# Side rows of the windowed distances: from four matmuls per group on tables built by three engines to one matmul of 316 columns on rows loaded from memory

## The reference, cut to what matters

```python
k_windows = q_h[:, idx, :]                 # the last 64 positions of every query
diff = k_windows - q_h[:, :, None, :]
dist = jnp.sqrt((diff * diff * m_h).sum(axis=-1) + 1e-08)
dist = jnp.where(mask[None], dist, jnp.inf)
neg_d, loc = jax.lax.top_k(-dist, K)       # K = 32
...
context = jnp.einsum('btk,btkd->btd', infl, neighbor_v)
```

## Time and profile before

| | us |
|---|---|
| median of 3 runs | 787.54 (785.96 to 788.2) |
| the profiled execution | 788.22 |
| its span | 786.4 |
| PE busy | 704.6 (90%) |
| DVE busy | 640.7 (81%) |
| POOL busy | 451.9 (57%) |
| ACT busy | 419.7 (53%) |

### The profile page before, as it was taken

How to read it: one execution, slowest core, us unless ns; L and a number is a source line. 1 busy time by engine, 2 the same in 40 slices (tenths; PEclk the granted TensorE clock), 3 DMA queues, 4 the chain that set the end, 5 groups by cost and what they waited for, 6 DMA issues and landing times.

```text
span 786.4 us, 11674 instructions
## 1 busy us (share of the span) xinstructions
PE 704.6 (90%) x3368; PEld 500.7 (64%) x3368; DVE 640.7 (81%) x2562; ACT 419.7 (53%) x757; POOL 451.9 (57%) x535
## 2 busy tenths in 40 slices
PE   3998999999999889999998999999998999978733
PEld 2645666666576666776676677666675776768623
DVE  3877787768999999849799999765799899659974
ACT  3754444566675555455675774456683754465300
POOL 2265366546676864854567856654668768433441
PEclk9979999999997999999998999999999999996555
DMA  9920000000000000000000000001000000010000
GB/s 287 358 68 1 1 0 0 2 1 16 17 1 10 9 15 11 9 15 20 13 1 8 11 12 16 8 7 26 14 2 9 10 15 15 19 31 8 18 23 17
DMA packets 25695, 22.14 MB, mean 28 GB/s; under 512 B 1892, under 2 KB 23424, under 8 KB 25120
## 3 DMA queue, kind: packets, MB, share of 16 engines
q1 hardware_dynamic: 25632, 21.40, 9.1%
HBM read 19.17 MB, written 2.23 MB: 27 GB/s over the span
## 4 chain that ended last, share of the span: by engine, by line
PE 44%; DVE 35%; POOL 7%; ACT 5%; issue 5%; DMA 4%; SPq 0%; DVEq 0%; POOLq 0%; ACTq 0%
PE bank_A L505 11%; PE bank_X L505 11%; PE bank_U L505 10%; PE bank_G L505 9%; DVE Wk L1193 8%; DVE S L790 6%; DVE m L1190 6%; DMA vw<-vscratch 4%; DVE GWk L790 2%; DVE sm L794 1%; POOL wT L1501 1%; POOL Wlo L1501 1%; ACT Ed L1259 1%; DVE wT L790 1%; ACT L1264 1%
## 5 line engine op out<-in xcount | busy, mean ns | idle before, releaser
L505 PE MATMUL bank_A<-S,WdT 128*128 128x512 f32 x368 | 186.8, 612 | 5.9 <-POOL S L1501 4.4
L1501 POOL TENSOR_TENSOR Wlo<-Wgu,Whi 128x256 fp32r<-128x256 f32 x138 | 108.3, 789 | 108.8 <-ACT Whi L1259 108.4
L790 DVE TENSOR_TENSOR S<-S,bank_U 128x512 f32<-128x512 f32 x184 | 123.7, 678 | 56.9 <-PE bank_U L505 36.0
L1259 ACT ACTIVATE S<-bank_G 128x512 f32<-128x512 f32 x184 | 108.2, 594 | 106.7 <-PE bank_G L505 98.0
L1501 POOL TENSOR_TENSOR S<-S,Rb 128x512 f32<-128x512 f32 x88 | 117.8, 1340 | 63.3 <-DVE S L790 59.3
L1259 ACT ACTIVATE Whi<-Wgu 128x256 fp32r<-128x256 f32 x184 | 74.0, 413 | 78.7 <-PE bank_U L505 69.8
L505 PE MATMUL bank_G<-xH,Whi 128*128 128x512 f32 x184 | 96.9, 526 | 5.5 <-POOL Wlo L1501 2.8
L505 PEld LDWEIGHTS bank_A<-S,WdT 128*128 128x128 f32 x368 | 66.7, 193 | 49.9 <-issue 29.2
L505 PE MATMUL bank_U<-xH,Whi 128*128 128x512 f32 x184 | 91.7, 498 | 5.0 <-DVE S L790 4.6
L790 DVE TENSOR_TENSOR S<-S,Rb 128x512 f32<-128x512 f32 x88 | 83.4, 951 | 2.4 <-ACT Rb L1259 0.5
L1193 DVE MATCH_REPLACE8 Wk<-m,Wk 128x79 f32<-128x79 f32 x384 | 81.8, 223 | 0.0
(11 more groups left out here) (233 smaller groups left out, 1440.9 us busy)
## 6 DMA issues: line engine op xcount, KB each, us to landing
vw<-vscratch SPq DMA_DIRECT2D x32, 158.0 KB
Wgu<-in_Wgu SPq DMA_DIRECT2D x2, 2048.0 KB, 15.3
xs<-in_x SPq DMA_DIRECT2D x4, 256.0 KB, 7.0
wqk<-in_w_qkv SPq DMA_DIRECT2D x1, 1024.0 KB, 7.3
Wgu<-in_Wgu SPq DMA_DIRECT2D x1, 1024.0 KB, 9.6
vscratch<-mo SPq DMA_DIRECT2D x4, 256.0 KB
out<-xs SPq DMA_DIRECT2D x3, 256.0 KB, 2.3
Wgu<-in_Wgu SPq DMA_DIRECT2D x1, 512.0 KB, 5.1
```

The lines of the kernel that those rows point to most:

```text
L505: return engine.matmul(dst, lhsT, rhs, start=start, stop=stop)
L790: return engine.tensor_tensor(dst, a, b, op)
L1259: return engine.activation(dst, src, f, bias=bias, scale=scale, accum_out=acc)
L1501: return engine.tensor_tensor(dst, a, b, op)
```

## The change

The queries' norms and the windows of key norms are no longer built by engines. Pk (now 8 rows) is stored to a scratch in DRAM, and for each group SP loads from it 4 rows of La (one per block, a piece of 16 values per head) and 8 rows of Ra (one per head, 4 windows of 79 values). La becomes one table of 28 rows and 128 columns for the whole group: 4 rows of query norms, 8 that pick the head, 16 that pick the query in the block. Ra has 28 rows of 4 by 79: 4 that are one in their own block only, 8 of key norms, 16 of the mask. PE issues one matmul of 316 columns, La against Ra, and then the four of Qb on top of it. `keys` on ACT is gone, and `operands` on DVE and POOL keeps Qb alone. SP gets a step `k`: the store of Pk, then two loads per group, from the third group on when the distances of the group two before are done. All strings of ORDER are written anew. The fixed rows of La and Ra come in 6 loads at the start in place of 4.

```diff
-AUX = 72
+AUX = GT + NH + TQ
...
     "sp":
-        "vvvvvvvvvsvvvvvvvvvsvvvvvvvvvsvvvvvsvvsvvss",
+        "vvvkkkkkkkkkvvvvvvsvvvkkkkkkkkkvvvvvvsvvvkkkkkkkkkvvvvvvvsvvkkkkkkkkvkvvsvvsvss",
...
+            def sides():
+                for b in range(B):
+                    yield
+                    sp.wait_ge(empty(bank("nm", b)), nth("nm", b) + 1)
+                    sp.wait_ge("pk", b + 1)
+                    load("st_p", pd[b], Pk[:, :])
+                    for g in range(NG):
+                        k, t0 = g % 2, g * GT * TQ
+                        yield
+                        if g == 0:
+                            sp.wait_ge("st_p", 16 * (b + 1))
+                        if g >= 2:
+                            sp.wait_ge(full(bank("dist", b, g - 2)), nth("dist", b, g - 2) + 1)
...
+                        q = pd[b, :, PADK + t0:]
+                        load(f"ld_s{k}", La[k][0:GT, :].rearrange("a (h t) -> a h t", h=NH),
+                             bass.AP(q.tensor, q.offset, [[TQ, GT], [PADK + T, NH], [1, TQ]]))
+                        q = pd[b, :, t0:]
+                        load(f"ld_s{k}", Ra[k][GT:GT + NH, :, :],
+                             bass.AP(q.tensor, q.offset, [[PADK + T, NH], [TQ, GT], [1, WK]]))
...
-                    pe.wait_ge("la_v" if not side else "la_p", side_count(not side, b, g))
-                    pe.wait_ge("ra", b * NG + g + 1)
+                    pe.wait_ge("qb_v" if queries_on_vector(b, g) else "qb_p", query_count(b, g))
+                    pe.wait_ge("ld_e", 96)
+                    pe.wait_ge(f"ld_s{k}", 32 * (b * (NG // 2) + g // 2 + 1))
+                    mm(t[:, 0:GT * WK], La[k][:, :], flat(Ra[k]), True, False)
                     for i in range(GT):
-                        o = t[:, WK * i:WK * i + WK]
                         w = slice(g * GT * TQ + TQ * i, g * GT * TQ + TQ * i + WK)
-                        mm(o, Qb[k][:, i, :], mk2[:, w], True, False)
-                        p = mm(o, La[k][:, i, :], Ra[k][:, i, :], False, True)
+                        p = mm(t[:, WK * i:WK * i + WK], Qb[k][:, i, :], mk2[:, w], False, i == GT - 1)
```

More of the change, by code:

```diff
@@ L73 @@
 _at = 0
-for _n, _w in (("ident", 128), ("bd", 128), ("tri", 64), ("neglo", 1), ("ones", 128), ("heads", AUX), ("pick", 128),
+for _n, _w in (("ident", 128), ("bd", 128), ("tri", 64), ("neglo", 1), ("ones", 128), ("heads", NH),
                ("eps8", 1), ("sel", 128)):
@@ L94, in constants @@
     h = np.arange(NH)
[L95 to L101, removed]
+    put("heads", p[:, None] // HD == h[None, :])
     put("sel", (p[:, None] % 16 == p[None, :] // 8) * 1.0)
@@ L317, in program @@
         hb = sb("hb", [64, 1])
-        nm72 = sb("nm72", [128, AUX])
-        Pk = sb("Pk", [AUX, PADK + T])
-        La = [sb(f"La{i}", [AUX, GT, 128]) for i in range(2)]
+        nm8 = sb("nm8", [128, NH])
+        Pk = sb("Pk", [NH, PADK + T])
+        La = [sb(f"La{i}", [AUX, 128]) for i in range(2)]
         Ra = [sb(f"Ra{i}", [AUX, GT, WK]) for i in range(2)]
@@ L376, in blocks_done, with queries_on_vector, query_count @@
             return b * NF + NF - NR + BLOCK * k + BLOCK - 1
-        def queries_on_vector(g):
+        def queries_on_vector(b, g):
             return g % 2 == 1
-        def side_count(on_vector, b, g):
-            return b * (NG // 2) + g // 2 + 1
+        def query_count(b, g):
+            on = queries_on_vector(b, g)
+            return sum(queries_on_vector(p, q) == on for p in range(B) for q in range(NG) if (p, q) <= (b, g))
         def last_side(b, g):
@@ L492, in stores @@
                             store(b, i, 1)
-            weave("sp", v=values(), s=stores())
+            weave("sp", v=values(), k=sides(), s=stores())
             sp.wait_ge("st_out", 16 * (B - 1 + NT))
@@ L1153, in operands @@
                     k, t0 = g % 2, g * GT * TQ
+                    if not queries_on_vector(b, g):
+                        continue
                     yield
@@ L1439, in head @@
                 if b > 0:
-                    sc_.wait_ge("ra", b * NG)
-                    sc_.wait_ge("la_p", b * NG // 2)
-                    sc_.wait_ge("la_v", b * NG // 2)
-                emptied(act(Pk[:, PADK:], t[0:AUX, :], ACT.Copy), "nm", b)
-            def keys(b):
-                for g in range(NG):
-                    k, t0 = g % 2, g * GT * TQ
-                    yield
-                    sc_.wait_ge("pk", b + 1)
-                    sc_.wait_ge("ld_e", 64)
-                    if g >= 2:
-                        sc_.wait_ge(full(bank("dist", b, g - 2)), nth("dist", b, g - 2) + 1)
-                    w = Pk[64:64 + NH, t0:t0 + WK]
-                    w = bass.AP(w.tensor, w.offset, [list(w.ap[0]), [TQ, GT], [1, WK]])
-                    act(Ra[k][64:64 + NH, :, :], w, ACT.Copy).then_inc(sems("ra"), 1)
+                    sc_.wait_ge("st_p", 16 * b)
+                emptied(act(Pk[:, PADK:], t[0:NH, :], ACT.Copy), "nm", b)
             def near(b):
@@ L1492, in scalar_engine @@
             weave("act", x=highs(), e=silus(), m=sums(), y=every(route), s=every(spreads), c=scales(), u=setup(),
-                  a=every(attend), f=every(dense), h=every(head), k=every(keys), n=every(near), g=every(gather))
+                  a=every(attend), f=every(dense), h=every(head), n=every(near), g=every(gather))
         def gpsimd_engine(engine):
```

118 lines of the change are left out of this document (54 added, 64 removed).

## The result

The changed kernel takes **813.8 us** (median of 4, 809.9 to 819.3) against 787.9 us for the kernel before beside it: a ratio of **1.034, 95% interval 1.026 to 1.041**. The forecast was 788.5 us and its range ended at 799, so it was wrong: slower, by some 26 us. The profiled execution took 817.1 us, its span is 815.3.

The account below looks back on a forecast made before the run. PE and DVE, both nearly full, bound the stretches beside the experts; serial window loads set the tail's end. Terms -8.6 - 2.4 - 3 + 7.5 + 1.5 + 1 + 5 = +1.0 gave 788.5 us as median, range 774 to 799.

Parts of the forecast that it names:

- The mechanism that it named: At batch heads, Pk's store and first side loads wait behind window loads, arriving 24.1 us after the values' store.
- PE's standstill: Before batch 2's first distances PE would stand 7.5 us waiting for side loads; batches 0 and 1 were covered.
- The third rival: Slower: from the third group on, every group waits on PE for its side loads; 801 us, chance 0.17.
- The standstill's price: Batch 2's head: 7.5 us of PE wait plus 1.5 us for a lower clock after it.
- what the change earns, -14 us: Beside the experts: savings of 8.6 us from PE's columns, 2.4 from the tables and 3 from the clock.
- PE's columns: One 316-column product at 0.53 us replaces four side products per group, saving 8.6 us over 24 groups, bounds 0.7 to 16.
- The clock's -3: Fewer, longer PE products beside the experts would win back 3 us of lost clock, bounds 0 to 8.6.
- the tables (-2.4): Table builds dropped from DVE, POOL and ACT would save 2.4 us of PE idle time, bounds 0 to 9.7.
- the tail, +5 us: After the experts, choosing starts 10.7 us later, leaner DVE regains part, and context 2 ends 5 us later.
- DVE's gain of 5.7 us: In the tail, DVE without table builds would get from first choice to context 2 in 30 us, before 35.7.
- four window loads carry every delay to the end: In the tail, four serial window loads take the 36 us to the end and pass on context 2's 5 us delay.
- the waits of later groups: From the third group on, pairs of side loads cost 0.3 us at three places a batch, 1 us in all.

Follow-up runs that it names:

- e1: Changed kernel, first two window loads of every batch cut into 64 and 15 rows: 800.5 us, ratio 1.016 to the kernel before.
- e5h: Changed kernel with engines in the order of the kernel before, first two window loads per batch cut into 64 and 15 rows: 796.5 us, ratio 1.010.
- e7n: Changed kernel, engines in the earlier kernel's order, 79-row windows, norm store and side loads on ACT's own queue: 801.3 us, ratio 1.014.
- e5e: Changed kernel, engines in the earlier kernel's order, without Pk's store and side loads (norms left out), 79-row windows: 780.2 us, ratio 0.989.
- e5ew: Changed kernel, engines in the earlier kernel's order, without Pk's store and side loads, all windows cut into 64 and 15 rows: 775.5 us, ratio 0.982.
- e3: Kernel before, with all window loads cut into 64 and 15 rows: 783.2 us, ratio 0.995.
- e2: Changed kernel, its own new order, all window loads cut into 64 and 15 rows: 794.2 us, ratio 1.005.
- e4: Changed kernel, its own new order, without Pk's store and side loads (norms left out): 805.7 us; one execution took 792.0.
- e5n: Changed kernel with engines in the order of the kernel before, all transfers kept, 79-row windows: 808.1 us, ratio 1.021.
- e5w: Changed kernel with engines in the order of the kernel before, all window loads cut into 64 and 15 rows: 793.5 us, ratio 1.004.
- e10w: Changed kernel, engines in the earlier kernel's order, windows cut into 64 and 15 rows, 316-column product behind its group's other four: 783.1 us, ratio 0.991.
- e12: e10w with one MLP product step moved ahead of the first distances on PE in batches 0 to 2: 782.5 us, ratio 0.991.
- e13: e12 with the attention-output step also moved ahead of the first distances in batch 3: 784.3 us, ratio 0.993.
- e8: e5w with the norms stored twice in each batch, the second store after the first has landed: 815.4 us, ratio 1.029.
- e7w: e7n with all window loads cut into 64 and 15 rows: 795.0 us, ratio 1.007.
- e9b: e5w without the norm store, side rows loaded straight from Pk in SBUF by five transfers a group: 812.8 us, ratio 1.024.

## Why the prediction was wrong

**The mechanism that it named was right.** The store lands under the window loads, and the first side tables were put at the values' store + 24.1: measured +24.8 from the values' store to the first distances of batch 3 (729.34 - 704.59), +25.1 in batch 2. PE's standstill was put in batch 2 alone of the first three, and it was there, 5.6 us for 7.5. The third rival, that every group waits for its loads, was not seen: only the heads wait. The Trainium skill, "DMA: Bandwidth & Descriptors", section "Why a DMA increments its semaphore by 16 and not by 1", has a DMA use the largest number up to 16 that divides its outermost sizes; by that 79 rows go on one engine and 64 on 16. The runs fit: cut into 64 and 15 rows the first windows let the norms through (e1, e5h), and without the cut not even another queue does (e7n, batch 3).

**The standstill's price was about right too.** The forecast had 7.5 us of wait and 1.5 of clock behind it, 9 in batch 2. Against e1, the same kernel with no wait there, batch 2 to 3 is 8.0 us longer for a wait of 5.6: 2.4 beyond its length, with a mean clock of 0.98 against 1.00. The 2.6 us for each us of the old-order runs is another case, of short waits at every head.

**First failed step: what the change earns, -14 us.** The largest term was PE's columns, -8.6. I took the proportion to the 512-column product, 0.53 us. It is 0.73 from start to next start, the other four cost 0.24 each instead of 0.22, and the term is 1.9 us, not far from its own lower bound of 0.7. The clock's -3 is nothing: from mo of batch 0 to mo of batch 3 the mean granted clock is 0.98 before, 0.98 in e5e and e5ew, and 0.97 in the changed kernel. With the tables (-2.4) the forecast had -14 us by the last head; e5e and e5ew, with nothing to fetch, have 2.9 and 4.2 (mo of batch 3 at 673.6 and 672.3 against 676.5). Over the whole kernel that gain is 8 us (e5e), and 10 us where both sides have wide windows (e5ew and e3, ratios 0.982 and 0.995, on different chips).

**Second, and not in the sum at all: the order.** I priced what is issued, not that every engine's order was written anew. Between batches 2 and 3 the new order takes 163.2 us with no wait for norms (e1, e2, e4), the old order with nothing to fetch 156.5 (e5e) and the kernel before 156.1: 7.1 us. The held store adds 8.0; together the 15.0 us. Which engine's string loses them no run separates.

**Third: the tail, +5 us.** It is +13.7. The first choice came 32.0 us after the values' store (736.57 - 704.59) where I had 28.7, and DVE's gain of 5.7 us was 1.1: from the first choice to the end are 78.7 us after and 79.8 before. Half of the 13.7 is the held store: e1, in the same order and with 0.2 us of such waits, has a tail of 116.5 us, 7.1 less than the changed kernel, and 6.6 more than before. In the old order the fetching alone makes as much: e5n's tail is 123.2 us, e5e's, with nothing to fetch, 107.6 and e5w's, with wide windows, 108.3. PE's waits for DMAs before (first line) and in e5n show that those for windows are the same and those for Ra came on top:

```profile
PE bank_U L505 <- DMA vw<-vscratch: 8.5, 2, 4.4
```
```profile
PE bank_G L524 <- DMA Ra<-pscratch: 12.6, 2, 10.0
PE bank_U L524 <- DMA vw<-vscratch: 8.4, 2, 4.4
```

The prediction also let four window loads carry every delay to the end, from two pieces of the chain of 15.4 and 15.0 us. PE's own waits for windows are 8.5 us in all, and without them the kernel before gains 0.5%, some 4 us (e3).

**The sum against the profile.** Forecast 789.2, measured 817.1, 27.9 us. By the values' store of batch 3: it came at 704.6 where the forecast's terms put it at 684.6 (688.6 - 14 + 7.5 + 1.5 + 1), 20.0 us; from there to the first choice 3.3; from there to the end 4.6. These add up to 27.9. Of the 20.0, 11.1 are the gain that e5e has not (2.9 for 14), 6.6 the order (mo of batch 3 in e1 against e5e, 680.3 and 673.6), and 2.0 less are the standstill and the waits of later groups, priced at 10 and found at 8.0. Then 4.3 are left: 3.5 by mo of batch 2 (520.6 against 517.1 in e1, where neither waits), and 0.8 from mo of batch 3 to the store.

The chance of 0.37 for slower was too low because the largest gain rested on a proportion and the new order had no term.

**What stays open.** Between e10w and e5ew, 0.9% or 7 us, waits of 4.5 us are left, but e12 and e13 took most of them away without gain. By the traces the difference lies in the tail: mo of batch 3 comes at 673.0 and 672.3, and the tails are 107.1 and 101.3. e12 and e13 have shorter tails too (103.5, 102.0), but reach that mo later (683.9, 678.8; the traced execution of e12 is its longest). Whether the rest is that the side product starts 4.3 us after the start of Pk's copy, or the 68 small transfers, no run tells. The kernel before on the new order was not run. A version that beats both kernels exists: e10w, 0.991 of the kernel before, and level with it e12; the kernel before with wide windows has 0.995. e10w and e3 ran on different chips and their intervals meet, so that the change is worth anything beyond the wide windows is not shown.

## What to carry to other kernels

Price a merged instruction by the start-to-start time of the whole group it sits in, not by columns. A small transfer that must be back before the bounding engine goes on is priced by that engine's standstill and by what the clock loses behind it (here 1.4 us in all for each us of one wait of 5.6, 2.6 for each us of waits of 0.6 to 4.5 at every head), and by the large transfers that are in flight beside it; see first that those are spread (64 + 15 rows instead of 79), then that the engine has work between asking and needing. And a schedule planned for a wait is a loss once the wait is gone: order and wait have to be judged together.

## What the runs showed of the hardware

- PE after a standstill: behind 3.0 to 3.3 us of idle the mean clock of the next ten us was 0.50 to 0.55 (e8, batches 0 to 2); behind 1.5 to 1.9 us it was 1.00 in six of nine cases and 0.83, 0.66 and 0.51 in the others (e7w, e5w, e7n). One trace each. It falls without a standstill too: 0.66 from 232 to 242 us in e5ew.
- The issue of a store behind two window loads is itself held on SP, 6.0 and 7.9 us (the changed kernel, batches 2 and 3), and takes 0.27 us where the windows have gone (e1).
- A load out of SBUF rows costs SP 0.62 to 0.78 us to issue (e9b), one out of memory 0.24 to 0.31 (the changed kernel), but for one of 1.98 issued in the tail behind a window load.
- A transfer on another engine's queue does not pass 79-row loads in flight: 5.2 us for a store (e7n) that takes 1.5 with wide windows (e5w).
- A 316-column float32 product holds PE at full clock for 0.73 us, 3.3 times the 0.22 of a 79-column one, with 4.0 times its columns (the changed kernel, the kernel before).
